# Value products of a 16-head attention with v packed as high and low halves, run one period later, in a chain of eight transformer blocks

## What is computed

```python
# block 0: gated feed-forward, twice (hidden 256, then 512)
x = x + gate * (gelu(norm(x) @ w1 + b1) @ w2 + b2)
# block 1: attention with HEADS, DH = 16, 64 and q, k, v from one matrix
qkv = x @ W_qkv
attn = softmax(einsum('bqhd,bkhd->bhqk', q, k) * DH ** -0.5)
out = einsum('bhqk,bkhd->bqhd', attn, v).reshape(B, T, 1024) @ W_out + b_out
x = x + g_msa * out                 # then a feed-forward, hidden 1024
# block 2: two feed-forwards (512), the first with masked rows
# block 3: attention with one head of width 256, then a feed-forward, hidden 1024
```

## Time and profile before

| | |
|---|---|
| median of 3 runs | 1777.46 us (1774.5 to 1777.64) |
| the profiled execution's own time | 1775.03 us |
| its span, first to last instruction | 1773.2 us |
| TensorE, VectorE, ScalarE, GpSimd busy | 95%, 68%, 64%, 57% |
| mean granted TensorE clock | 0.98 |

### The profile page before, as it was taken

The page is one execution under the profiler, slowest core; times in us unless marked ns, Lnnn a source line. Parts: engine busy times, 40 slices in busy tenths (PEclk is TensorE's granted clock), DMA queues, the critical chain, the costliest instruction groups (busy, mean ns, idle before and its releaser), DMA issues.

```text
span 1773.2 us, 38293 instructions
## 1 busy us (share of the span) xinstructions
PE 1683.8 (95%) x13763; PEld 1522.2 (86%) x13763; DVE 1204.0 (68%) x2830; ACT 1129.4 (64%) x2828; POOL 1003.6 (57%) x1141
## 2 busy tenths in 40 slices
PE   4888989999999999999999889999999989989997
PEld 2557879999999999999999779999888889979997
DVE  3757857777777777777777745555888768864442
ACT  3445647677767676767777655556676657766663
POOL 1555757766767676767676623333555568842223
PEclk7899999999999999999999989999999999999999
DMA  9112310000000000000000011110212112220111
GB/s 305 54 51 85 85 44 11 11 10 2 11 11 11 11 11 11 10 11 11 11 10 11 1 31 31 31 31 19 60 56 58 44 28 46 46 52 30 42 49 48
DMA packets 110975, 65.98 MB, mean 37 GB/s; under 512 B 81530, under 2 KB 92788, under 8 KB 110788
## 3 DMA queue, kind: packets, MB, share of 16 engines
q1 hardware_dynamic: 110788, 63.54, 13.2%
HBM read 59.06 MB, written 4.46 MB: 36 GB/s over the span
## 4 chain that ended last, share of the span: by engine, by line
PE 86%; DVE 5%; issue 3%; ACT 2%; POOL 2%; DMA 1%; POOLq 0%; DVEq 0%; SPq 0%; ACTq 0%
PE bank L252 25%; PE bank L253 23%; PE bank L254 23%; PE bank L989 5%; PE bank L1045 5%; PE bank L380 3%; PE bank L440 1%; DVE xn L339 1%; DVE stats L316 1%; ACT bank L393 1%; ACT nThi L393 1%; POOL x L627 1%; ACT bank L573 0%; DVE nTlo L401 0%; DMA x<-in_x 0%
## 5 line engine op out<-in xcount | busy, mean ns | idle before, releaser
L1027 POOL TENSOR_SCALAR prob<-prob,rinv 128x256 f32<-128x256 f32 x512 | 464.8, 925 | 211.0 <-DVE rinv L1021 211.0
L573 ACT ACTIVATE hh<-bank,vecs 128x512 fp32r<-128x512 f32 x240 | 166.9, 696 | 280.5 <-PE bank L254 279.4
L579 DVE TENSOR_TENSOR hl<-bank,hh 128x512 fp32r<-128x512 f32 x240 | 163.5, 684 | 199.2 <-ACT bank L573 198.1
L1012 ACT ACTIVATE prob<-bank,nmax 128x256 f32<-128x256 f32 x512 | 238.4, 475 | 4.2 <-DVE nmax L1002 4.1
L1055 ACT ACTIVATE pthi<-bank 128x512 fp32r<-128x512 f32 x256 | 139.1, 595 | 135.8 <-PE bank L1045 135.8
L252 PE MATMUL bank<-WBhi,hl 128*128 128x256 f32 x768 | 217.5, 283 | 1.1 <-DVE upd L610 1.0
L253 PE MATMUL bank<-WBlo,hh 128*128 128x256 f32 x768 | 216.4, 282 | 0.0
L254 PE MATMUL bank<-WBhi,hh 128*128 128x256 f32 x768 | 216.1, 281 | 0.0
L1060 DVE TENSOR_TENSOR ptlo<-bank,pthi 128x512 fp32r<-128x512 f32 x256 | 175.1, 684 | 23.0 <-ACT pthi L1055 23.0
L1002 DVE TENSOR_REDUCE nmax<-bank 128x2 f32<-128x512 f32 x256 | 174.7, 683 | 20.2 <-PE bank L989 19.2
L252 PE MATMUL bank<-aThi,WAlo 128*128 128x256 f32 x576 | 176.9, 307 | 6.8 <-POOLq L242 6.8
(11 more groups left out here) (164 smaller groups left out, 5185.2 us busy)
## 6 DMA issues: line engine op xcount, KB each, us to landing
gates<-gate_scratch SPq DMA_DIRECT2D x96, 256.0 KB, 3.5
agate<-gate_scratch SPq DMA_DIRECT2D x32, 256.0 KB, 3.7
stage<-in_L_cond_W SPq DMA_DIRECT2D x64, 64.0 KB, 2.3
out<-x SPq DMA_DIRECT2D x16, 256.0 KB, 2.2
adaw<-in_L_cond_Wc SPq DMA_DIRECT2D x1, 3072.0 KB, 17.7
stage<-in_L_cond_W_qkv SPq DMA_DIRECT2D x8, 384.0 KB, 3.4
x<-in_x SPq DMA_DIRECT2D x1, 2560.0 KB, 16.8
stage<-in_L_cond_ff_w SPq DMA_DIRECT2D x32, 64.0 KB, 2.1
```

Of the source, the lines that this page charges most:

```text
L573: last = act.activation(dst[:, :], U_BANKS[r][:, :], ACTF[p], bias=vecs[:, at:at + 1])
L579: dve.tensor_tensor(hl[r][:, :], U_BANKS[r][:, :], hh[r][:, :].bitcast(F32), ALU.subtract).then_inc(h_lo, 1)
L1012: last = act.activation(prob[h % 4][:, q, :], SB_[h % 2][:, q * SEQ:(q + 1) * SEQ], ACT.Exp, bias=nmax[h % 4][:, q:q + 1], accum_out=rsum[ ...
L1027: last = pool.tensor_scalar(prob[h % 4][:, q, :], prob[h % 4][:, q, :], rinv[h % 4][:, q:q + 1], None, ALU.mult)
```

## The change

v is packed: each head has 128 columns, its high and its low 64 (`v_heads`), in one tile `vv`. A head's product is now 2 times 2 passes, with `ptlo` and with `pthi`, and gives the part from v's high half in 64 partitions and the part from its low half in the other 64. A pair fills the whole bank `OB`. ScalarE copies the parts from the low half across (`o_read`, into `oc`), VectorE adds them (`o_add`, into `of`) and rounds (`oThi`), and GpSimd makes `oTlo` (`o_rest`). Value products run one period later and output projections three periods behind the transposes. `pt` has four buffers instead of two. The maxima of a pair are one instruction over two banks, and so are its reciprocals. In the last two pairs ScalarE weighs one head of two. The four common ends of stages are gone, and each engine waits for what it needs (`after_ff`, `after_attention`). In feed-forward 0 transposes go ahead of the hidden product, the output is taken a group later, and the slices of stage 1 are read earlier.

```diff
@@ tiles
-        VP = 3 * DH
-        vv = [sb(f"v{k}", [P, TPB, PAIRS * VP], F32R, att) for k in ("hi", "lo")]
+        VP = 4 * DH
+        vv = sb("vv", [P, TPB, PAIRS * VP], F32R, att)
+        of = sb("of", [P, SEQ], scope=att)
+        oc = sb("oc", [P, SEQ], scope=att)
-        pt = [[sb(f"pt{k}{i}", [P, 2 * SEQ], F32R, att) for k in ("hi", "lo")] for i in range(2)]
+        pt = [[sb(f"pt{k}{i}", [P, 2 * SEQ], F32R, att) for k in ("hi", "lo")] for i in range(4)]
@@ stage ends
+        def after_ff(name, eng, p):
+
+            if name == "tensor":
+                eng.wait_ge(w_lo, SLICE_BASE[p + 1])
+                eng.wait_ge(h_lo, CHUNK_BASE[p])
+            if name == "scalar":
+                eng.wait_ge(u_mm, CHUNK_BASE[p])
+            if name == "gpsimd":
+                eng.wait_ge(x_new, GB * GROUP_BASE[p])
@@ slices_of, ff_body
+            if C <= GB:
+                return [[(1, 0)], [(0, 1), (1, 2)], [(0, 3), (1, 4)], [(1, 5)], [(1, 6)], [(1, 7)], [], []][g]
...
-                        for u in units if C > GB and c == 0 else []:
+                        for u in (units if c == 0 else []) if C > GB else units[c:c + 1]:
                             ln_unit(name, eng, *u)
                         if nxt:
                             ff_hidden(eng, *nxt)
-                        for u in units[c:c + 1] if C <= GB else []:
-                            ln_unit(name, eng, *u)
...
-                        if c == 0 and prev and chunks(prev[0]) > GB:
+                        if c == 0 and prev:
                             ff_take(eng, *prev)
-                        if c < len(units) and C > GB:
+                        if last_norms and c == 1:
+                            for n in norms:
+                                ln_norm(eng, *n)
+                        if c < len(units):
                             ln_unit(name, eng, *units[c])
...
-                        if own_take and c == C - 1:
-                            ff_take(eng, p, g, i)
@@ score_max
-            dve.tensor_reduce(nmax[h % 4][:, :], SB_[h % 2][:, :].rearrange("p (q k) -> p q k", q=TPB), AX_X, ALU.max,
-                              negate=True).then_inc(nmax_ready, 1)
+            dve.tensor_reduce(nmax[n % 2][:, :], s_banks[:, :, :].rearrange("p h (q k) -> p (h q) k", q=TPB), AX_X, ALU.max,
+                              negate=True).then_inc(nmax_ready, 2)
@@ head_values
-            if h % 2 == 0 and H:
-                pe.wait_ge(o_lo, H // 2)
-            i, at = h // 2 % 2, h // 2 * VP + h % 2 * DH
+            if h % 2 == 0 and H:
+                pe.wait_ge(o_sum, H)
             for c in range(TPB):
-                last = split3(pe, OB[:, i * SEQ:(i + 1) * SEQ], [m[:, c, at:at + P] for m in vv],
-                              [m[:, c * SEQ:(c + 1) * SEQ] for m in pt[h % 2]],
-                              c == 0 and h % 2 == 0, c == TPB - 1 and h % 2 == 1)
+                for m in (1, 0):
+                    last = pe.matmul(OB[:, h % 2 * SEQ:(h % 2 + 1) * SEQ], vv[:, c, h * P:(h + 1) * P],
+                                     pt[h % 4][m][:, c * SEQ:(c + 1) * SEQ],
+                                     start=c == 0 and m == 1, stop=c == TPB - 1 and m == 0, skip_group_check=True)
@@ o_read, o_add, o_rest
-            act.activation(oT[i][0][:, :], OB[:, i * SEQ:(i + 1) * SEQ], ACT.Copy).then_inc(o_hi, 1)
+            for j in range(2):
+                main, rest, cols = o_halves(j)
+                act.activation(oc[main, :], OB[rest, cols], ACT.Copy).then_inc(o_corr, 1)
+        def o_add(dve, pair, i):
+            if pair:
+                dve.wait_ge(o_lo, pair)
+            for j in range(2):
+                main, _, cols = o_halves(j)
+                dve.wait_ge(o_corr, 2 * pair + 2)
+                dve.tensor_tensor(of[main, :], OB[main, cols], oc[main, :], ALU.add).then_inc(o_sum, 1)
+            dve.wait_ge(o_sum, 2 * pair + 2)
             if pair >= 2:
-                act.wait_ge(out_mm, pair - 1)
+                dve.wait_ge(out_mm, pair - 1)
+            dve.tensor_copy(oT[i][0][:, :], of[:, :]).then_inc(o_hi, 1)
+        def o_rest(pool, pair, i):
+            pool.wait_ge(o_hi, pair + 1)
+            pool.tensor_tensor(oT[i][1][:, :], of[:, :], oT[i][0][:, :].bitcast(F32),
+                               ALU.subtract).then_inc(o_lo, 1)
@@ mh_tensor
             if n:
-                out_project(pe, n - 1, (n - 1) % PAIRS, (n - 1) // PAIRS)
-            for h in range(2):
-                head_values(pe, b, 2 * j + h)
+                values_pair(pe, n - 1)
             if n == PERIODS - 1:
-                out_project(pe, n, j, b)
+                out_pair(pe, n - 2)
+                values_pair(pe, n)
+                ff_hidden(pe, A + 1, 0, 0, 1)
+                out_pair(pe, n - 1)
+                out_pair(pe, n)
@@ mh_vector
             if n + 1 < PERIODS:
-                for h in range(2):
-                    prob_inverse(dve, 2 * n + 2 + h)
-            if j == 1 and b:
+                prob_inverse(dve, n + 1)
+            if j == 3 and b:
                 res_vector(dve, A, b - 1, YB, out_mm, PAIRS * b, b - 1)
-            if n:
-                o_rest(dve, n - 1, (n - 1) % 2)
+            if n + 2 < PERIODS:
+                score_max(dve, n + 2)
+            if n >= 2:
+                o_add(dve, n - 2, n % 2)
             for h in range(2):
-                if n + 2 < PERIODS:
-                    score_max(dve, 2 * n + 4 + h)
                 pt_rest(dve, 2 * n + h)
@@ mh_gpsimd
-            if n + 1 < PERIODS:
+            if n + 1 < PERIODS - SHARED:
                 prob_weigh(pool, 2 * n + 3)
+            if n >= 2:
+                o_rest(pool, n - 2, n % 2)
```

257 lines of the change are left out of this document (153 added, 104 removed).

## The result

The changed kernel takes 1749.99 us (median of 4 runs, 1748.74 to 1754.28) against 1776.26 us before (4 runs, 1774.5 to 1777.64). The ratio is 0.9857, with an interval of [0.9837, 0.9877]: faster by 26 us. The forecast was 1716 us with a range from 1684 to 1744, so it had the sign right, and more than half of the 58 us did not come.

A forecast was written before the change was run, and what follows sets the result against it. TensorE, busy 95% of the span, was taken as the bound, with VectorE's chain limiting four of eight attention periods after the change. 1775.0 - 25 (attention) - 20 (stage ends) - 13 (feed-forward 0) = 1717; predicted 1716, range 1684 to 1744.

The forecast's parts named there:

- -7: End of the 16-head attention: of 10 us idle and the clock lost, 7 us would be gained.
- the wait of 4.33 for the weighing: Behind the 16-head attention: TensorE's 4.33 us wait disappears, with norms four periods earlier and ScalarE taking a head.
- 5.05: Attention periods without v, j = 0 and 7: VectorE's chain sets 5.05 us from start to start, a gain of 0.11.
- 11.35: Attention periods j = 3 and 4 together: rinv slips by 0.5, so 11.35 us instead of 10.85, a loss.
- VectorE already makes PE wait here: Attention periods j = 3 and 4 before the change: TensorE was said to wait for VectorE's late rinv.
- 6.08: Four attention periods per sequence with v: TensorE sets 6.08 us instead of 6.56, gaining the full 0.48.
- Rival 3: Attention: GpSimd holds VectorE's rounding copy, at 1.38 us, making the kernel slower, 1790 us; chance 0.03.
- Rival 1: Attention: TensorE stays the bound, periods without v take 4.68 us, gain 61 instead of 25, 1681 us; chance 0.15.
- -13: Feed-forward 0: total gain of 13 us, bounds -5 and -20.
- the wait of 4.59 goes, as its slices end two groups earlier: Feed-forward 0: the 4.59 us wait for the last low weights at 138.15 us disappears.
- But the output is now taken a group later and the conditioning step keeps its place: Feed-forward 0: the reason given for counting only 13 us beside waits of 11.9 and 4.59 us.
- rival 2: The attention gains nothing; only stage ends and feed-forward 0 remain, 1742 us, or 1750 where ends give less; chance 0.19.

The follow-up runs named there:

- e4: Changed kernel, with the conditioning step's stores and loads between the two weight loads of a group in SyncE's queue (feed-forward 0): 1750.04 us.
- e5: Changed kernel, with the conditioning step's stores and loads ahead of each weight load used only in a later group, groups 3 and 4 too (feed-forward 0): 1742.83 us.
- e12: Changed kernel with feed-forward 0's order of transposes, outputs and slices put back as in the kernel before: 1753.31 us.
- e3: Changed kernel, with the next stage's first statistics kept in j = 3 of the last sequence but rstd and xn moved to j = 4: 1745.25 us.
- e6: Changed kernel, with the norms of feed-forward 3's second group made in the last attention period, ahead of VectorE's last two additions: 1747.43 us.
- e9: Changed kernel with five edits together (e1, e2, e3, e5, e6): 1708.39 us.
- e2: Changed kernel, with VectorE making a pair's reciprocals earlier, ahead of the projections' low parts, statistics and normalized rows: 1746.56 us.
- e1: Changed kernel, with VectorE's rounding copy oThi behind both ptlo of its period instead of ahead of them: 1730.0 us.
- e7: Changed kernel with the edits of e1 and e2 together: 1726.63 us.
- e8: Changed kernel with the four common ends of stages put back, the order of work staying as changed: 1762.47 us.

## Why the prediction was wrong, point by point

In the traces 37.3 of the forecast 58 us are missing: 14.3 at the end of the 16-head attention, 11.3 in its periods, 9.6 in feed-forward 0 and 2.1 at the other ends.

- **The end of the 16-head attention: "-7" came as +7.3** (+4.3 to +5.1 in e4, e5 and e12). The step that failed is "the wait of 4.33 for the weighing [...] goes (norms four periods earlier [...])". The norms moved two periods, from j = 5 to j = 3, and still stand between the two weighings of one period, so the wait moved with them and became 6.37 us. With `rstd` and `xn` a period behind their statistics it became 2.11 and 1.25 (e3, 3.9 us in these periods). The forecast did name normalized rows as "late next", but those of the first group and at less than what goes; it is the second group's `xn` that costs 5.22 us of wait, and TensorE works at half the clock behind it (e6 gives 2 to 3 us of that). Waits for the additions (1.29 and 1.23 us) were not in the forecast. Even with both edits (e9) n = 116 to the third group of feed-forward 3 takes 102.6 us against 105.9 before, though the eleven periods have 0.48 us less of passes each. So the -7 was too much there in any case, and what the rest would need stays open.
- **The mechanism of the attention was right, its size was not** (13.7 us measured; 25 forecast, 23 of them in these rows). The terms that were too small are the periods without v. The steps "5.05" for j = 0 and 7 gave 5.13 to 5.46 and 5.28: the chain starts 0.1 us later and ends in transposes 0.1 later, and the copy that I priced at 0.42 takes 0.29 to 0.63. The step "11.35" for j = 3 and 4 gave 11.70. It rests on "VectorE already makes PE wait here", which is too strong: before, the weighing ended at 629.93 (3.63 us from 626.30) and the transposes started at 629.98 with no idle time in their row, so the two were level. But from there a slip counts in full, and it was 0.73, not 0.5. The step "6.08" holds for j = 1, 5 and 6, but j = 2 takes 6.16, since its `rinv` stands behind the statistics of the next sequence (e2, with `rinv` ahead of them, has 6.06) and GpSimd's `rstd` between the weighings. Together 46.56 us per sequence instead of 45.8, and half of the small gain of 1.6 was gone. e1 shows that the limit is the chain ahead of `ptlo`; e2 and e7 show the second one, `rinv` and the weighing, close behind. Whether two maxima between the two `ptlo`, as before, would do better than the one ahead of both was not tried. Passes of 0.12 us, additions of 0.42 and `oTlo` at 0.73 us came as priced. The two additions take 0.86 us and the copy starts only 0.03 us behind them (582.64), while `qklo` starts 0.06 us before the end of `ptlo`; the rule of the Trainium skill (VectorE: DVE Perf Modes, "Two Vector instructions with no wait between them") fits that, though the copy's own wait on a semaphore would give the same. Rival 3 is out: no copy took over 0.63 us. Rival 1's floor of 4.68 was not reached even in e7 (4.80).
- **Feed-forward 0: "-13" measured 3.4** (3.3 in e12). The step "the wait of 4.59 goes, as its slices end two groups earlier" was true, and so was that the waits of 1.98 go. "But the output is now taken a group later and the conditioning step keeps its place" was priced at 3.5 us (11.9 + 4.59 against 13). The later output alone makes TensorE wait 1.55 and 3.52 us. And I followed the moved slices on VectorE and GpSimd, but not in SyncE's queue, where they hold the biases of the conditioning step, which costs TensorE 4.61 us. e5 removes that wait, for 5 us in its trace and 7 by the medians.
- **The other ends were right:** -5.75 against -6, and -5.2 against -7 for the two later ones (-6.9 to -7.9 in e4, e5 and e12); e8 shows that the signs are most of it.
- **The range** had its upper end from an attention that gains nothing (rival 2, 1742 to 1750). The attention gained half of its forecast; the ends and feed-forward 0, whose bounds were -10 and -5 at the least, gave 7 us together. The measured 1750 has rival 2's number and a part of its mechanism (periods j = 7, 0, 3 and 4 longer than counted); the larger part of the miss lies outside the attention's periods.

## What to carry to other kernels

Price a moved instruction in every queue that it enters, the DMA queue above all: behind a load that waits for a free buffer stand loads that wait for nothing. A queue in order makes the place of the waiting instruction the question: one set of norms between two weighings held TensorE for 6.37 us, longer than any of the common signs had (4.34 us at most), and moving it to an earlier period did not help as long as it stood between them. Before giving a wait up as gone, look at what stands ahead of the instruction that ends it in the new order. And when one engine becomes nearly as busy as the bound (VectorE 90% of these sequences), reorder it so that what others wait for comes first; here two reorderings without any less work gave 23 us.
